# Last eight experts' combine weights: stored to memory and read back as broadcast rows

## The reference, cut to what matters

```python
# x: (8, 1024, 128) f32; mixer (gated linear attention with normaliser) and layernorm first, then:
g = sigmoid(x @ gate_w.T)                       # 16 experts
topv, topi = top_k(g, 4)
combine = zeros(T, 16).at[t, topi].add(topv / sum(topv))
h = silu(x @ e_win[e]) * (x @ e_vin[e]) * combine.T[e, :, None]     # (16, T, 64)
routed = einsum('eth,ehd->td', h, e_wout)
shared = silu(x @ ws_in) * (x @ vs_in) @ ws_out
out = layernorm(x + shared + routed)
```

## Time and profile before

| | us |
|---|---|
| median of 3 runs (841.82 to 844.51) | 843.5 |
| the profiled execution | 842.96 |
| its span, first to last instruction | 841.2 |
| PE busy | 782.8 (93%) |
| DVE busy | 666.0 (79%) |
| POOL busy | 378.4 (45%) |
| ACT busy | 363.0 (43%) |

### The profile page before, as it was taken

One profiled execution on the slowest core, in us unless ns is written; L12 is line 12 of the kernel. 1 busy time (PEld: TensorE's weight loads), 2 busy tenths in 40 slices (PEclk: granted clock), 3 DMA queues, 4 the chain that ended last, 5 costly groups with the idle time before them and its releaser, 6 DMA issues.

```text
span 841.2 us, 17387 instructions
## 1 busy us (share of the span) xinstructions
PE 782.8 (93%) x5805; PEld 662.4 (79%) x5805; DVE 666.0 (79%) x1719; ACT 363.0 (43%) x637; POOL 378.4 (45%) x370
## 2 busy tenths in 40 slices
PE   6977987799999999999999999999999999999976
PEld 5655776687888888888888888888888888888855
DVE  5697989787888787878787878787878787878754
ACT  4666787623434333343434343434343333434131
POOL 6040466163545454645454545454545454543200
PEclk8798999999999999999999999999999999999978
DMA  4688375600414040404040404040404040401000
GB/s 124 189 256 267 127 247 184 238 26 26 121 51 138 26 137 25 137 25 137 25 137 25 137 25 137 25 137 25 137 25 137 25 137 25 137 25 27 1 13 14
DMA packets 53435, 81.14 MB, mean 96 GB/s; under 512 B 10496, under 2 KB 37272, under 8 KB 49432
## 3 DMA queue, kind: packets, MB, share of 16 engines
q1 hardware_dynamic: 53400, 80.68, 31.2%
HBM read 55.24 MB, written 25.43 MB: 96 GB/s over the span
## 4 chain that ended last, share of the span: by engine, by line
PE 68%; DVE 16%; issue 8%; ACT 4%; SPq 2%; DMA 2%; POOL 1%; DVEq 0%; POOLq 0%; ACTq 0%
PE bank L1686 12%; PE bank L1657 8%; PE bank L1661 7%; PE bank L1658 7%; PE bank L1604 6%; PE bank L1602 4%; PE bank L1609 4%; PE bank L1630 3%; PE bank L1676 3%; DVE st L1214 3%; DVE acc L1018 3%; PE bank L1573 2%; PE bank L1645 2%; DVE Y L1226 2%; PE bank L1620 2%
## 5 line engine op out<-in xcount | busy, mean ns | idle before, releaser
L879 ACT ACTIVATE s_in<-bank 128x512 f32<-128x512 f32 x144 | 86.2, 599 | 175.6 <-PE bank L1661 173.4
L1686 PEld LDWEIGHTS bank<-ewout,h 128*128 128x128 f32 x1024 | 133.5, 192 | 9.1 <-DVE h L1349 0.2
L1686 PE MATMUL bank<-ewout,h 128*128 128x128 f32 x1024 | 135.4, 275 | 0.0
L1345 DVE TENSOR_TENSOR h<-s_in,bank 128x512 f32<-128x512 f32 x144 | 98.1, 681 | 44.1 <-PE bank L1661 32.4
L1657 PE MATMUL bank<-yT_hi,in_hi 128*128 128x512 f32 x288 | 127.8, 444 | 0.3 <-DVE run_max L1104 0.2
L633 POOL TENSOR_TENSOR rs<-ve,half 128x4 f32<-128x4 f32 x32 | 32.6, 1018 | 210.6 <-DVE ve L1222 210.6
L1661 PE MATMUL bank<-yT_lo,in_hi 128*128 128x512 f32 x288 | 115.2, 400 | 0.0
L1658 PE MATMUL bank<-yT_hi,in_lo 128*128 128x512 f32 x288 | 114.7, 398 | 0.0
L1349 DVE TENSOR_TENSOR h<-h,bank 128x512 f32<-128x512 f32 x128 | 87.1, 681 | 14.5 <-PE bank L1676 14.5
L619 POOL TENSOR_TENSOR D<-a_tok,max_b 128x512 f32<-128x512 f32 x64 | 67.5, 1076 | 61.3 <-DVE max_b L1132 31.3
L648 POOL TENSOR_TENSOR kept<-state,decay 128x260 f32<-128x260 f32 x64 | 40.9, 638 | 115.1 <-DVE state L1175 114.9
(11 more groups left out here) (198 smaller groups left out, 1625.8 us busy)
## 6 DMA issues: line engine op xcount, KB each, us to landing
xact_scratch<-xact SPq DMA_DIRECT2D x16, 1024.0 KB, 5.2
max_b<-max_scratch SPq DMA_DIRECT2D x15, 1024.0 KB, 7.4
xa<-xact_scratch SPq DMA_DIRECT2D x16, 512.0 KB, 6.1
silu_z<-xact_scratch SPq DMA_DIRECT2D x16, 512.0 KB, 3.8
inter_w<-inter_scratch SPq DMA_DIRECT2D x30, 256.0 KB, 7.0
x_in<-in_L_attn_x_dram SPq DMA_DIRECT2D x16, 256.0 KB, 5.8
xt_scratch<-x_t SPq DMA_DIRECT2D x16, 256.0 KB, 5.9
xT<-xt_scratch SPq DMA_DIRECT2D x16, 256.0 KB, 7.9
```

Source lines behind the costliest of these rows:

```text
L879: act.activation(s_in[:, j % 2], bank[4][:], ACT.Silu).then_inc(silu_done, 1)
L1345: dve.tensor_tensor(dst[:, j % 2], s_in[:, j % 2], bank[5][:], ALU.mult).then_inc(h1_done, 1)
L1686: i = pe.matmul(bank[7][:, k * P:(k + 1) * P], h2[:, j % 2, k * P:(k + 1) * P], w, start=(j == k == 0), stop=(j == NJ), skip_group_check=True)
```

## The change

For pairs 1 to 4 (`NJ_MM` = 4, experts 0 to 7) nothing changes in kind. For pairs 5 to 8 (experts 8 to 15) PE makes no product; the transposed weights go to a scratch tensor in memory and come back as rows broadcast over 64 partitions each, in `row_b`, from which DVE reads them.

```diff
+    weight_d = nc.dram_tensor("weight_scratch", [NG, NX - NX_MM, G], F32).ap()
+        full_rows = sb("full_rows", [3 * NX, G])
-        comb = sb("comb", [P, NC, NX])
-        comb2 = sb("comb2", [P, NC, 2 * NX], F32R)
+        comb3 = sb("comb3", [P, NC, 3 * NX])
+        row_b = sb("row_b", [P, 2, (NX - NX_MM) // 4, G])
# SP, in mix, after load_xa(g + 1); in mix(15) and in the last feed-forward before the store of the output
+                    if f is not None:
+                        weight_rows(f)
+            def weight_rows(f):
+                sp.wait_ge(combT_out, f + 1)
+                alone(sp)
+                sp.dma_start(weight_d[f], full_rows[2 * NX + NX_MM:]).then_inc(weight_stored, 16)
+                prev(sp, h2_done, f, NJ)
+                alone(sp)
+                sp.wait_ge(weight_stored, 16 * (f + 1))
+                alone(sp)
+                for i in range(2):
+                    for t in range(2):
+                        rows = weight_d[f].rearrange("(i n t) x -> i t n x", i=2, t=2)[i, t]
+                        sp.dma_start(row_b[t * HX:(t + 1) * HX, i], rows.partition_broadcast(HX)).then_inc(row_in[i], 16)
# ACT, slot 2
-                    prev(act, bc_mm, f, NJ)
-                    copy(combT[0:2 * NX], bank[6][0:2 * NX, :]).then_inc(combT_out, 1)
+                    prev(act, bc_mm, f, NJ_MM)
+                    prev(act, weight_stored, f, 16)
+                    copy(combT[0:2 * NX], bank[6][0:2 * NX, :])
+                    copy(full_rows[2 * NX:], bank[6][2 * NX:3 * NX, :]).then_inc(combT_out, 1)
# DVE; comb and comb2 are now slices of comb3
+            comb, comb2 = comb3[:, :, 2 * NX:], comb3[:, :, 0:2 * NX].bitcast(F32R)
-                    dve.wait_ge(bc_mm, nth(f, NJ, j - 2))
-                    dve.tensor_tensor(h2[:, (j - 1) % 2], h1[:, (j - 1) % 2], bank[6][:], ALU.mult).then_inc(h2_done, 1)
+                    if j - 1 <= NJ_MM:
+                        dve.wait_ge(bc_mm, nth(f, NJ_MM, j - 2))
+                        row = bank[6][:]
+                    else:
+                        i, n = divmod(j - 2 - NJ_MM, 2)
+                        dve.wait_ge(row_in[i], 32 * (f + 1))
+                        dve.wait_ge(out_mm, nth(f, NJ, j - 3))
+                        row = row_b[:, i, n]
+                    dve.tensor_tensor(h2[:, (j - 1) % 2], h1[:, (j - 1) % 2], row, ALU.mult).then_inc(h2_done, 1)
# PE
+                alone(pe)
-                    i = pe.transpose(bank[6][0:2 * NX, k * P:(k + 1) * P], comb2[:, k].bitcast(F32), ident[:])
+                    i = pe.transpose(bank[6][0:3 * NX, k * P:(k + 1) * P], comb3[:, k], ident[:])
-                if j == NJ:
-                    i.then_inc(o_mm, 1)
+                i.then_inc(o_mm if j == NJ else out_mm, 1)
-                if 2 <= j <= NJ + 1:
+                if 2 <= j <= NJ_MM + 1:
                     combine_rows(f, j - 1)
+NJ_MM = 4
+NX_MM = 8
```

More of the change, by code:

```diff
@@ L307, in mixer_moe_block @@
         bc_mm, h2_done = sem("bc_mm"), sem("h2_done")
+        out_mm = sem("out_mm")
+        weight_stored, row_in = sem("weight_stored"), sems("row_in", 2)
         o_mm = sem("o_mm")
@@ L541, in mix @@
                         late(7)
+                if isinstance(g, int) and g == NG - 1:
+                    weight_rows(f)
                 if f is not None:
@@ L548, in mix, with last @@
                     late_xact(LATE)
+            def weight_rows(f):
[10 more added lines that the diff above has]
+                        sp.dma_start(row_b[t * HX:(t + 1) * HX, i], rows.partition_broadcast(HX)).then_inc(row_in[i], 16)
+            def last(f):
+                weight_rows(f)
+                store(f)
             def store(f):
@@ L556, in ready @@
                 sp.wait_ge(rows_stored, 32 * HALVES * NC)
-            groups(sp, mix, store, ready)
+            groups(sp, mix, last, ready)
             sp.wait_ge(out_stored, 16 * NG)
@@ L1326, in routing @@
                     after(8)
-                    dve.tensor_tensor(comb[:], chosen[:], crec[:].unsqueeze(2).to_broadcast([P, NC, NX]), ALU.mult
+                    dve.tensor_tensor(comb, chosen[:], crec[:].unsqueeze(2).to_broadcast([P, NC, NX]), ALU.mult
                                       ).then_inc(route, 1)
@@ L1331, in routing @@
                     after(9)
-                    dve.tensor_copy(comb2[:, :, 0:NX], comb[:]).then_inc(route, 1)
+                    dve.tensor_copy(comb2[:, :, 0:NX], comb).then_inc(route, 1)
                     after(10)
-                    dve.tensor_tensor(comb2[:, :, NX:], comb[:], comb2[:, :, 0:NX].bitcast(F32), ALU.subtract
+                    dve.tensor_tensor(comb2[:, :, NX:], comb, comb2[:, :, 0:NX].bitcast(F32), ALU.subtract
                                       ).then_inc(route, 1)
```

## The result

The changed kernel took 848.9 us (median of 12 runs, 847.26 to 854.67), the kernel before 844.09 (12 runs beside them, 840.52 to 846.25): a ratio of 1.0071, 95% interval 1.005 to 1.0091. It is slower by 4.8 us by the medians and by 6.0 by the ratio of the runs. The forecast of 845.4 was +1.9 against its own median. Its range held the result and the direction was my likeliest of three at 0.42, but the rise is 2.5 times the one that I gave as the single number. The profiled execution took 851.49 us (span 849.8), 8.6 more than the one of before.

The account below looks back on a forecast made before the run. PE's stream was taken to set the time. An ordinary group summed to -0.48 + 0.6 + 0.1 + 0.06 = +0.28 us; in all 3.6 - 0.3 - 0.56 - 0.8 = +1.9, 845.4 us against the median, range 833 to 852.

Parts of the forecast that it names:

- The products of slots 6 and 7: PE, before H and vin(8): removing 2 x 0.24 us gains 0, since both wait for other engines; bounds 0 to 0.48.
- Slots 8 and 9, -0.48: PE, late in the group: each removed product gives 0.24 us per group and passes it on; bounds 0.3 to 0.56.
- h2(5) and the boundary, +0.6: DVE and POOL: h2(5) runs between `hn` and `qs`, delaying `qs`, L1207 and h1(7); 0.6 us per group, bounds 0 to 0.9.
- Rival A: DVE and POOL: h2(5) neither waits nor pushes `qs`; group about -0.35 us, 837.2 us in all; chance 0.13.
- ACT's second copy, +0.1: ACT, at `combT_out`: the second copy makes PE's first product 0.1 us later per group; bounds 0.05 to 0.25.
- `alone` and the wider transposes, +0.06: PE, before the weights' transposes: `alone(pe)` costs 0.06 us per group, bounds 0 to 0.12; 48 instead of 32 columns cost 0.
- The transfers, 0: SP's queue: the store and four broadcast loads land in time, cost 0 with 3.7 us in hand.
- Rival C: Row loads take twice the time, `row_in[0]` lands at about 452 and h2(5) falls behind `qs`; chance 0.03.
- g = 1, -0.3: Group 1: DVE's scan steps keep L1207 away from `qs`, so -0.48 + 0.16 = -0.3 us.
- The end, -0.8: Last feed-forward: the last `ffn_out` begins its loads 0.95 us sooner, + 0.16, giving -0.8 us.
- Rival B: POOL wins the boundary and h2(5) stands until `qs` ends: +2.0 us per group instead of +0.6, 862 in all; chance 0.12.
- Rival D: PE: the whole removed product time comes back, 0.96 us per group, -13 us in all, 830; chance 0.08.

Follow-up runs that it names:

- late_qs: Changed kernel with one added GpSimd wait, so that `qs` starts only after the group's last h2: 842.41 us, ratio 0.9985.
- two_exact: Changed kernel with only pairs 7 and 8 from memory and `qs` after the last h2, both ACT copies kept: 837.3 us, ratio 0.9916.
- kept: Changed kernel with all eight products still made on PE, while DVE reads the rows for pairs 5 to 8: 855.52 us, ratio 1.0165.
- late_h2: Changed kernel with h2(5) also waiting for the first half of H, so it is issued after `qs` begins: 866.03 us (two runs), ratio 1.0267.
- one_copy: Changed kernel with ACT copying all 48 rows at once and the store reading from there, last eight experts' weights rounded: 843.58 us, ratio 1.0008.
- rows_first: Changed kernel with SP issuing the row transfers ahead of the scan's stores and loads in group 2 only: 847.02 us, ratio 1.0054.
- pair5_pe: Changed kernel with pair 5's product back on PE, pairs 6 to 8 still reading rows: 839.04 us, ratio 0.9945.
- two_pairs: Changed kernel with only pairs 7 and 8 from memory, products of pairs 5 and 6 back on PE: 842.26 us, ratio 0.9988.
- before_late_qs: Control: the kernel before the change, with `qs` moved after the last h2: 840.96 us, ratio 0.9976.
- all2: Changed kernel with both `qs` after the last h2 and a single ACT copy of all 48 rows: 837.63 us, ratio 0.9926.
- before: The kernel before the change, unedited: 844.09 us.

## Why the prediction was right, and where it was off

- **The products of slots 6 and 7 are worth nothing: right to 0.02.** `late_qs` and `two_exact` have 42.08 and 42.10.
- **Slots 8 and 9, -0.48: nearly.** `kept` says -0.39, inside the bounds of 0.3 to 0.56.
- **h2(5) and the boundary, +0.6: right.** 0.57 by `late_qs`, of which 0.03 to 0.07 was there before. `qs` grew from 2.39 to 2.91 (I had named 3.0), L1234's pair from 1.34 to 1.87 (I had named 1.9). Rival A is out: the lengths changed and `late_qs` undid them. That h2(5) won is in part luck. The forecast had it 0.12 us ahead of `qs`; in nine of twelve groups it was 0.03 or less, and `late_h2` shows the price of losing. One reading behind it was wrong: of the two rows given for a set-back POOL only that of `x_lo` shows one, for beside the 8-element L1188 the two L619 take their usual 2.04. On the rule weighed in the forecast: by the Trainium skill ("SBUF — State Buffer", "Who interferes with whom") the ports that VectorE and GpSimd share are an exclusive lock, and issue order decides who blocks. `late_h2` agrees in numbers, with 2.04 us for an h2 of 0.68.
- **ACT's second copy, +0.1: the mis-sized term of an ordinary group.** 0.29 by `one_copy`, above my upper bound of 0.25. I took the distance of two copies from the earlier trace rows, 0.49, where it is 0.60 here, and let the delay end at the first product, while 0.1 more arose before H.
- **`alone` and the wider transposes, +0.06: right.** From the Y transposes to the start of those of the weights it is 10.93 us, 10.85 before: +0.08. PE's load side is idle for 0.18 us just before them, 0.12 before. From there to the first product it is 1.83 us in `one_copy` and 1.84 before, so that the 48 columns add nothing that shows. No run takes `alone` out.
- **An ordinary group:** -0.39 + 0.54 + 0.29 + 0.08 = 0.52 against a measured 0.45 and a forecast 0.28. The 0.07 left over no run explains.
- **The transfers, 0: right in the ordinary groups, the step that failed in group 2.** "Here the queue is empty but for `xa`" does not hold there. `rows_first` gives back 1.25 of the 1.44 us. Rival C was the right danger with the wrong cause: the loads aren't slow (a median of 4.4 us from issue to landing, my row of `inter_w` said 6.4), they are issued late.
- **g = 1, -0.3: wrong in sign, its cause in part open.** DVE there:

```profile
190.86 1.02 DVE L1385 TENSOR_TENSOR h<-h,row_b 128x512 f32<-128x512 f32 x1
...
191.80 2.55 DVE L1114 TENSOR_TENSOR_SCAN carry_rows<-end_rows,carry_rows 32x4 f32<-32x4 f32 x2
```

and PE, which waits for that scan:

```profile
194.40 0.24 PE L1811 MATMUL bank<-carry_rows,ident 32*32 32x2 f32 x8 [1.93 <-DVE carry_rows L1114]
```

Before, that wait was 1.48. h2(5), held to 1.02 by `hn`, pushes the carry scan behind it: 0.45 us. With h2(5) back on PSUM the wait is 1.48 again (`pair5_pe`, `two_pairs`). The scan itself is held by `qs`, in the kernel before too, which the forecast missed: it takes 2.44 us there and 0.46 once `qs` is late, and g = 1 then takes 46.07 (`before_late_qs`) and 46.12 (`late_qs`). The rest of the 1.8 goes with the place of a stretch at the 1.2 GHz level. Before, it comes right after the wait of 1.48: the mean granted clock from 194 to 200 is 0.72. `rows_first`, whose code in this group is that of the changed kernel, has it there too (0.72 from 191 to 197), waits 0.89 us for DVE afterwards and takes 48.60. In the changed kernel's profile the clock is 1.00 until 200; PE waits 2.02 us for DVE at 197, is busy 0.98 of the 3 us to 200, and has a mean clock of 0.57 from 200 to 204, behind that wait: 49.82. Each run here whose g = 1 is above 47.5 has such a stretch in it, and none under 47.2 has. So 1.2 us of the rise differ between runs of the same code; what moves the stretch is open.

- **g = 15, -0.56: right,** -0.54.
- **The end, -0.8: right at equal clock.** From slot 3's `ffn_in` to the last instruction it is 24.57 us against 25.52: -0.95. Ahead of it both kernels fall to the 1.2 GHz level after the idle time between the last group and the last feed-forward. The changed one, back at 2.4 GHz by 819 (PE busy 1.24 us of 3 until 822), fell a second time:

```profile
822.08 0.63 PE L1693 MATMUL bank<-yT_hi,in_hi 128*128 128x512 f32 x1
822.50 0.63 PE L1694 MATMUL bank<-yT_hi,in_lo 128*128 128x512 f32 x1
```

These starts are 0.42 apart, 0.23 in the same place before, and the whole last part took 39.64 us for 38.96. The second fall doesn't follow from the change alone: `late_qs` and `rows_first` run the same last feed-forward, stay at 2.4 GHz there and take 38.20 and 38.22, which is some 0.75 less than before. It is in `one_copy`, `all2` and `late_h2` again, and in none of `before`, `before_late_qs` and `kept`; what decides is open.
- **Rival B, +2.0 per group for a blocked h2(5): right in size.** In `late_h2` the end of h2(5) is set by `qs`, as it would be in B, and against `late_qs`, where nothing contends, the group is 44.03 - 42.08 = 1.95 longer. Its condition, that POOL wins, did not occur; in most groups h2(5) was ahead by 0.03 us or less. Rival D is out with the first point.

Between the two profiles, my 13 groups of +3.6 became 4.7 + 1.4 = 6.1, g = 1 +1.8 for -0.3, the end +0.7 for -0.8. The medians' 4.8 to 6.0 are less than the profiles' 8.6. In `rows_first` g = 1 and the end take 2.6 us less than in the changed kernel's profile with the same code; that is of the size of the difference, but only the profiled executions show it. The rise in the ordinary groups is the part that the experiments settle.

## What to carry to other kernels

Count a removed TensorE product only where nothing behind it, before the engine's next release by another engine, is awaited anyway: of 0.96 us removed per group 0.39 came back. Before an operand moves from PSUM to SBUF, look at what GpSimd runs at that moment and what is queued behind it, and move that (here `qs`, two lines, 0.57 us per group). And a new transfer has to be checked in each special iteration of the issuing queue's stream, not in the typical one alone.

## What the runs showed that I had not expected

- A VectorE instruction that starts only 0.00 to 0.03 us before GpSimd's next one still gets in between two instructions queued there back to back; GpSimd's loses 0.52 us (2.39 to 2.91). Issued 0.89 us after it, the same operation takes 2.04 us for 0.68. The contention costs 0.57 us per group on the one side of that boundary (`late_qs`) and 44.03 - 42.69 = 1.34 on the other. Where between 0.03 ahead and 0.89 behind the boundary lies, no run shows.
- A copy out of PSUM by ACT takes 0.59 us with 16, 32 or 48 rows of 512 elements; splitting one costs a whole one.
- `qs` can start 7 us later at no cost, and in the kernel with rows this is worth more (0.57 us) than all four products removed (0.39). It also takes 2.0 us off g = 1 of the kernel before (48.03 to 46.07), where `qs` holds a scan on DVE's chain.
